# A decoder layer on one core: the attention steps of a quad taken chunk by chunk instead of pair by pair

## Chip, core and metric

The kernel runs on one core of a Trainium2 chip. The metric is the device time of one execution in microseconds (us). Engines are named as in the profile: PE is TensorE (PEld its weight loads), DVE is VectorE, ACT is ScalarE, POOL is GpSimd, SP is SyncE, which only issues DMAs here.

## What is computed

A decoder layer on x of 16 batches x 128 tokens x 1024, in three stages, each behind a layer norm and with a residual: latent attention with 32 heads (rotary part included), cross attention to a context, and a feed-forward stage of three layers with signed weights. The change touches the first stage alone. Cut to that stage:

```python
c_q = hidden_states @ w_q_down                    # 1024 -> 384
q_nope = (c_q @ w_q_up_nope)...                   # 32 heads x 128
q_rope = rope((c_q @ w_q_up_rope)...)             # 32 heads x 64
c_kv = hidden_states @ w_kv_down                  # 1024 -> 128, keys and values of all heads
k_rope = rope(hidden_states @ w_k_rope)
q_lat = einsum('bhsd,hdr->bhsr', q_nope, wuk)     # latent query, 128 per head
scores = q_lat . c_kv + q_rope . k_rope           # causal, softmax
out_lat = einsum('bhst,btr->bhsr', probs, c_kv)
out = einsum('bhsr,hdr->bhsd', out_lat, wuv)... @ w_out
x = x + out
```

## The kernel before, in words

`transform` is the first stage. Tokens lie in four chunks of 512 (`CHUNKS`, four batches each), two chunks make a group (`CPG` = 2, `GROUPS` = 2). Heads lie in eight quads of four heads, a quad in two pairs. Every large product is made in three matmul passes of split operands (`three_passes`, lines 66 to 70: high x high, high x low, low x high), so nearly every result leaves PSUM twice: ACT copies the high part out, DVE subtracts it to make the low part.

**Preparation** (PE lines 621 to 646). For each of four chunks in the order 2, 3, 0, 1, and each of eight slices `k` of 128 columns, PE transposes a slice two ahead (`turn_x`, bank `prep_turned`) and multiplies the current one into five banks (`project`, m = 0 to 4: three banks of queries `c_q`, one of keys, one of rope keys). ACT and DVE split each transposed slice into `hT_hi`, `hT_lo` (three slices of room) and, after `k` = 7, empty the five banks into `tok`. `BESIDE` puts other work at the end of some (chunk, k): the absorbed weights of the first heads (`"A"`: w_q_up_nope times w_uk of a pair, `"B"`: w_uv times w_out of one head), the rope queries of chunk 0 and its first latent queries. `load_w_down` brings the projection weights in four equal pieces of two slices; ACT cuts the high part (`cut_w_down`, 720), POOL the low part (894).

**Opening** (PE 648 to 663). What has to be ready before the loop: rope queries of the second chunk, the first two score tiles, two more latent queries, the first turned probabilities and values.

**Quads.** `quads` (247) runs the slots: quads 0 to 6 in a loop ("full", group 0, and they absorb the weights of the next quad and store them), quad 7 ("switch", tokens of group 1 are loaded), quads 8 to 14 in a loop ("later", group 1, weights loaded back), the last quad ("last"). A quad has eight steps; step s is one pair of heads, one chunk, and two of its four batches. `place(s)` (222) says which: before, pair 0 takes steps 0 to 3 (chunk 0, then chunk 1), pair 1 steps 4 to 7. In slot s PE issues, strictly in this order (`slot`, 665): turn of the probabilities of step s+1, scores of s+2, output of s (first batch), a latent query for two units ahead, values of s+1, output of s (second batch), then in two slots of a quad (`ROPE_AT`) the rope queries of the next quad, and in six of them (`ABSORB`) a piece of weights to absorb. ACT (861), POOL (934) and DVE (1150) follow the same slots in an order of their own.

**The two query banks.** Latent queries, rope queries and absorbed weights all go through two PSUM banks `qbank`, used in turn and numbered by `USE`: use n is written to bank n mod 2, and may start once use n-2 has been read out by DVE. Each reader adds 1 to the semaphore `q_taken` per use, with one exception: DVE's `rope` (1043 to 1056) reads both banks of a rope (uses n+1, n+2) in four products with cosine and sine, and adds 2 after the last of them:

```python
times(0, 0, cos)
times(1, 1, sin)
times(2, 0, sin)
times(3, 1, cos).then_inc(q_taken, 2)
```

PE's waits: `rope` waits for `taken` and `taken + 1` before its halves (558), `absorb_head` for `taken + n` before half n (542), `latent` for `taken` (548).

SP issues all DMAs in one order written out by hand (`preparation` 327, `full_quad` 390, `switch_quad` 414, `later_quad` 459): raw weights go into two ring buffers, absorbed weights to DRAM, rope queries through DRAM and back (`relayout`, 280), tokens and weights of group 1 back from DRAM.

Of the kernel before, what the change touches and what calls it, by code (L numbers as in the profile page):

```python
# [23 lines left out]
F32R = mybir.dt.float32r  # L24
# [6 lines left out]
P = 128  # L31
# [8 lines left out]
PAIR = 2  # L40
# [32 lines left out]
def transform(nc, x, w_down, w_heads, w_rope, consts, scratch, x1_d):  # L73
# [14 lines left out]
    PIECES, SLICES = 4, 3  # L88
# [3 lines left out]
    ROPE_AT = {2: 0, 4: 1}  # L92

    turns = [("x", 0), ("x", 1)]
    for g in range(KT * N):
        if g + 2 < KT * N:
            turns.append(("x", g + 2))
        if g % KT == 2 and g > KT:
# [6 lines left out]
              (3, 1): ("rope", 0), (3, 3): ("latent", 0), (3, 4): ("latent", 1)}  # L105
# [4 lines left out]
    USES_PREPARED, USES_OPENING, USES_FULL, USES_SWITCH, USES_LATER = 8, 8, 24, 16, 12  # L110

    ctx = ExitStack()
    with ctx:
# [19 lines left out]
        wqr = sb("at_wqr", [P, 2, WQR_W], F32R)  # L133

# [5 lines left out]
        pT_hi = sb("at_pT_hi", [P, CH], F32R)  # L140
        pT_lo = sb("at_pT_lo", [P, CH], F32R)
# [4 lines left out]
        with ExitStack() as early:  # L146
# [8 lines left out]
            stats = sb("pj_stats", [P, BPC, 2, 6], of=early)  # L155
# [6 lines left out]
        qlat1 = sb("at_qlat1", [P, 2, PAIR, CH], F32R)  # L162
# [5 lines left out]
        nmax = [sb(f"at_nmax{i}", [P, PARTS]) for i in range(2)]  # L168
        sums = [sb(f"at_sums{i}", [P, PARTS]) for i in range(2)]
        rsum = [sb(f"at_rsum{i}", [P, PARTS]) for i in range(2)]  # L170
# [14 lines left out]
        w_in = [sem(f"pj_w_in{j}") for j in range(PIECES)]  # L185
# [36 lines left out]
        def place(s):  # L222

            return (s // 2) // CPG % 2, (s // 2) % CPG
# [5 lines left out]
        def first_use_later(m):  # L230
# [3 lines left out]
        USE = {"full": [3 * s for s in range(STEPS)], "switch": [0, 3, 6, 9, 10, 13, 14, 15],  # L234
               "later": [0, 1, 2, 5, 6, 9, 10, 11], "last": [0, 1, 2, 3]}
# [4 lines left out]
        ABSORB = {0: ("B", 2, 0, 0), 1: ("B", 3, 0, 2), 3: ("A", 0, 1, 4), 5: ("B", 0, 1, 6), 6: ("B", 1, 1, 8),  # L240
                  7: ("A", 2, 1, 10)}
# [17 lines left out]
        def absorbed(kind, s):  # L259
            if kind == "full":  # L260
                return ABSORB.get(s)
            return ABSORB[s] if kind == "switch" and s < 2 else None

# [5 lines left out]
        def _(sp):  # L269
# [53 lines left out]
            def load_w_down(j):  # L323
                rows = slice(j * KT // PIECES, (j + 1) * KT // PIECES)
                sp.dma_start(w_raw[:, rows, :], w_down[:, rows, :]).then_inc(w_in[j], 16)

            def preparation():
# [4 lines left out]
                for t in range(BPC):  # L332
                    load_x_tile(0, t)
                load_w_down(0)
# [55 lines left out]
            def full_quad(q):  # L390

                parts, uses = USES_PREPARED + 12 * q, first_use(q)
                load_raw_rope(q + 1)
                sp.wait_ge(ab_mm, parts + 2)
                load_pair(q + 1, 0, 0)
                store_wqr(q + 1)
                sp.wait_ge(ab_mm, parts + 4)
                load_head(q + 1, 0, 1)
                store_wvo(q, 1, uses + USE["full"][1] + 3)
# [1403 lines left out]
```

## Time and profile before

| | |
|---|---|
| median of three runs | 2170.99 us (2170.54 to 2172.58) |
| the profiled execution | 2170.82 us |
| its span in the profile | 2168.7 us |
| mean granted PE clock | 0.985 |
| PE busy | 2088.7 us, 96% of the span, 10688 matmuls |
| DVE busy | 1278.7 us, 59% |
| ACT busy | 712.3 us, 33% |
| POOL busy | 361.9 us, 17% |

The span is the time from the first to the last instruction that the profiler saw; 2.1 us of the execution lie around it. Busy times of the engines overlap. In the timeline, the two numbers of a row are start and duration; matmuls are pipelined, so the next one starts before the record of the one before ends, and what a matmul costs the engine is the distance of two starts. A slot of a full quad is named by its step.

### The profile page before, as it was taken

The numbers are of one execution on the slowest core, as the hardware profiler recorded it, in microseconds if no ns is written. First come the engines' busy times: TensorE is split into PE (matmuls) and PEld (weight loads), VectorE is DVE, ScalarE is ACT, GpSimd is POOL, SyncE is SP. The second block draws the span as 40 slices with busy tenths as digits, with TensorE's granted clock in tenths as the row PEclk, the third lists the DMA queues.
The fourth block names the chain that finished last, engine by engine and source line by source line (L and its number), as shares of the span: only waits on it lengthen the run. The fifth ranks groups of instructions, "written<-read, shape, count | busy, mean of one in ns | idle before, by whom it ended". The sixth has DMA issues, their size and how long they took to land. (4 is left out here: it accounts for less than half of the span.)

```text
span 2168.7 us, 29831 instructions
## 1 busy us (share of the span) xinstructions
PE 2088.7 (96%) x10688; PEld 1741.3 (80%) x10688; DVE 1278.7 (59%) x2122; ACT 712.3 (33%) x1911; POOL 361.9 (17%) x316
## 2 busy tenths in 40 slices
PE   6998999999999999999999999999998869999999
PEld 4786888888888888888888888888887647888887
DVE  4645666666666666666666666666665764233322
ACT  3323343333333343333333333233332223232321
POOL 2011212122121212021121211212110114000000
PEclk9998999999999999999999999999999888999999
DMA  5624353543535443666433434324332971012000
GB/s 189 239 84 140 129 180 118 175 147 121 181 121 165 134 144 128 218 239 244 158 92 106 131 129 137 107 91 141 132 95 83 391 304 59 39 39 78 1 39 39
DMA packets 66695, 297.47 MB, mean 137 GB/s; under 512 B 6992, under 2 KB 7888, under 8 KB 55248
## 3 DMA queue, kind: packets, MB, share of 16 engines
q1 hardware_dynamic: 66640, 296.72, 39.5%
q8 instruction: 37, 0.61, 0.1%
q14 instruction: 18, 0.15, 0.0%
HBM read 179.25 MB, written 117.44 MB: 137 GB/s over the span
## 5 line engine op out<-in xcount | busy, mean ns | idle before, releaser
L1088 DVE TENSOR_TENSOR at_acc<-at_out,at_acc 128x512 f32<-128x512 f32 x512 | 351.8, 687 | 92.7 <-PE at_out L70 86.3
L70 PE MATMUL at_out<-at_wvo,at_val_lo 128*128 128x512 f32 x1024 | 401.5, 392 | 0.0
L68 PE MATMUL at_out<-at_wvo,at_val_hi 128*128 128x512 f32 x1024 | 401.1, 392 | 0.0
L69 PE MATMUL at_out<-at_wvo,at_val_hi 128*128 128x512 f32 x1024 | 400.7, 391 | 0.0
L787 ACT ACTIVATE at_probs<-at_probs,at_nmax 128x128 f32<-128x128 f32 x512 | 199.6, 391 | 419.9 <-DVE at_nmax L1066 419.9
L907 POOL TENSOR_TENSOR at_probs<-at_probs,at_rsum 128x512 f32<-128x512 f32 x128 | 133.4, 1042 | 857.3 <-DVE at_rsum L1071 857.3
L70 PEld LDWEIGHTS at_out<-at_wvo,at_val_lo 128*128 128x128 f32 x1024 | 192.7, 188 | 41.8
L68 PEld LDWEIGHTS at_out<-at_wvo,at_val_hi 128*128 128x128 f32 x1024 | 193.3, 189 | 32.5 <-DVE at_acc L1088 0.6
L69 PEld LDWEIGHTS at_out<-at_wvo,at_val_hi 128*128 128x128 f32 x1024 | 192.9, 188 | 31.4
L1697 PE MATMUL ff_lin<-ff_act_hi,ff_w 128*128 128x512 f32 x512 | 200.5, 392 | 6.1 <-DVE ff_act_lo L1632 6.1
L1698 PE MATMUL ff_lin<-ff_act_lo,ff_w 128*128 128x512 f32 x512 | 199.9, 390 | 0.0
L793 ACT ACTIVATE at_pT_hi<-at_turned 128x512 fp32r<-128x512 f32 x128 | 76.4, 597 | 322.3 <-PE at_turned L593 322.3
L586 PE MATMUL at_score<-at_tok,at_qrope 128*128 128x256 f32 x512 | 171.3, 335 | 0.0
L584 PE MATMUL at_score<-at_tok,at_qlat 128*128 128x256 f32 x512 | 154.8, 302 | 1.8 <-DMA at_qrope<-parts_d 1.8
L68 PE MATMUL at_qbank<-at_tok,at_wabs 128*128 128x512 f32 x384 | 151.2, 394 | 2.1 <-DVE at_rope_tmp L1049 2.1
L69 PE MATMUL at_qbank<-at_tok,at_wabs 128*128 128x512 f32 x384 | 151.6, 395 | 0.0
L70 PE MATMUL at_qbank<-at_tok,at_wabs 128*128 128x512 f32 x384 | 150.1, 391 | 0.0
L1639 DVE TENSOR_TENSOR ff_act_lo<-ff_hid,ff_act_hi 128x512 fp32r<-128x512 f32 x64 | 45.1, 708 | 174.1 <-ACT ff_act_hi L1587 174.1
L1040 DVE TENSOR_TENSOR at_qlat<-at_qbank,at_qlat 128x512 fp32r<-128x512 f32 x128 | 88.2, 689 | 88.8 <-ACT at_qlat L773 88.8
L914 POOL TENSOR_TENSOR at_rope_tmp<-at_rope_tmp 128x512 f32<-128x512 f32 x64 | 81.5, 1295 | 327.0 <-DVE at_rope_tmp L1049 327.0
L1697 PEld LDWEIGHTS ff_lin<-ff_act_hi,ff_w 128*128 128x128 f32 x512 | 96.6, 189 | 27.2 <-DVE ff_act_lo L1632 7.2
L585 PE MATMUL at_score<-at_tok,at_qlat 128*128 128x128 f32 x512 | 114.2, 223 | 0.0
(150 smaller groups left out, 3916.9 us busy)
## 6 DMA issues: line engine op xcount, KB each, us to landing
wvo_d<-at_wvo SPq DMA_DIRECT2D x16, 2048.0 KB, 8.0
parts_d<-at_rope_parts SPq DMA_DIRECT2D x32, 1024.0 KB, 6.4
at_qrope<-parts_d SPq DMA_DIRECT2D x128, 256.0 KB, 5.2
at_wvo<-wvo_d SPq DMA_DIRECT2D x16, 2048.0 KB, 8.4
ab_raw<-in_w_heads SPq DMA_DIRECT2D x32, 576.0 KB, 4.4
cr_ctx_raw<-in_context SPq DMA_DIRECT2D x16, 1024.0 KB, 9.2
wabs_d<-at_wabs SPq DMA_DIRECT2D x16, 768.0 KB, 7.0
at_wabs<-wabs_d SPq DMA_DIRECT2D x16, 768.0 KB, 7.7
```

Source lines behind the costliest of these rows:

```text
L68: pe.matmul(out, w_hi, x_hi, start=first, stop=False)
L69: pe.matmul(out, w_hi, x_lo, start=False, stop=False)
L70: return pe.matmul(out, w_lo, x_hi, start=False, stop=last)
L584: pe.matmul(score[:, j], q_hi, keys[:, :, cols], start=True, stop=False)
L585: pe.matmul(score[:, j, 0], q_lo, keys[:, 0, cols], start=False, stop=False)
L586: ins = pe.matmul(score[:, j], qrope[c][:, pair * PAIR + h, cols], rope_keys[:, :, cols], start=False, stop=True)
L787: ins = act.activation(probs[i][:, j, :], probs[i][:, j, :], ACT.Exp, bias=nmax[i][:, j:j + 1], accum_out=sums[i][:, j:j + 1])
L907: pool.tensor_tensor(probs[i][:], probs[i][:], rsum[i][:].unsqueeze(2).to_broadcast([P, PARTS, SEQ]), ALU.mult).then_inc(probs_ready, 1)
L1040: dve.tensor_tensor(qlat[u % 2][:, 1, h, :], qbank[use % 2][:], as_f32(qlat[u % 2][:, 0, h, :]), ALU.subtract).then_inc(q_taken, 1)
L1088: dve.tensor_tensor(at, outb[n][:], at, ALU.add).then_inc(added, 1)
L1697: pe.matmul(lin[m % 2][:], wk, act_hi[at][:, k, :], start=k == 0, stop=False)
L1698: ins = pe.matmul(lin[m % 2][:], wk, act_lo[at][:, k, :], start=False, stop=k == KT - 1)
```

## The change

The steps of a quad go chunk by chunk: both pairs on chunk 0 (steps 0 to 3), then both on chunk 1. With it:
- `ROPE_AT` puts the second rope of a quad behind slot 5 instead of slot 4, and `ABSORB` the six pieces behind slots 0, 3, 4, 5, 6, 7 instead of 0, 1, 3, 5, 6, 7. Slot 5 now has both, a rope and a head to absorb; `absorbing` gives the piece the bank uses behind those of the rope.
- The latent queries of both pairs on chunk 0 are made in the preparation (`BESIDE`), none in the opening; the opening absorbs head 2 of the first quad.
- The opening is put in another order on all engines.
- In the preparation, `turn_x` for two slices ahead is issued ahead of the slice's five projections instead of behind the first of them, and queries are emptied after the transposed slice.
- The projection weights come in pieces of 1, 1, 2 and 4 slices, the first right behind the first tile of x.
- SP's orders follow; some tiles lie elsewhere in SBUF; the small statistics share one tensor.

The diff, cut (places of tiles, and DVE's and ACT's loops where they repeat PE's, are left out):

```diff
-    PIECES, SLICES = 4, 3
+    SLICES = 3
+    PIECES = (slice(0, 1), slice(1, 2), slice(2, 4), slice(4, KT))
-    ROPE_AT = {2: 0, 4: 1}
+    ROPE_AT = {2: 0, 5: 1}
     BESIDE = {(0, 4): ("A", 0), (0, 6): ("A", 1), (1, 4): ("B", 0), (1, 6): ("B", 1),
-              (3, 1): ("rope", 0), (3, 3): ("latent", 0), (3, 4): ("latent", 1)}
+              (3, 1): ("rope", 0), (3, 3): ("latent", 0), (3, 4): ("latent", 1),
+              (3, 5): ("latent", 2), (3, 6): ("latent", 3)}
-    USES_PREPARED, USES_OPENING, USES_FULL, USES_SWITCH, USES_LATER = 8, 8, 24, 16, 12
+    USES_PREPARED, USES_OPENING, USES_FULL, USES_SWITCH, USES_LATER = 8, 10, 24, 14, 12
...
         def place(s):
-            return (s // 2) // CPG % 2, (s // 2) % CPG
+            return s // 2 % 2, s // UNITS % CPG
...
-        USE = {"full": [3 * s for s in range(STEPS)], "switch": [0, 3, 6, 9, 10, 13, 14, 15],
-               "later": [0, 1, 2, 5, 6, 9, 10, 11], "last": [0, 1, 2, 3]}
+        USE = {"full": [0, 3, 4, 7, 10, 13, 18, 21], "switch": [0, 3, 4, 7, 8, 9, 12, 13],
+               "later": [0, 1, 2, 5, 6, 7, 10, 11], "last": [0, 1, 2, 3]}
-        ABSORB = {0: ("B", 2, 0, 0), 1: ("B", 3, 0, 2), 3: ("A", 0, 1, 4), 5: ("B", 0, 1, 6), 6: ("B", 1, 1, 8),
-                  7: ("A", 2, 1, 10)}
+        ABSORB = {0: ("B", 3, 0, 0), 3: ("A", 0, 1, 1), 4: ("A", 2, 1, 2), 5: ("B", 0, 1, 3), 6: ("B", 1, 1, 4),
+                  7: ("B", 2, 1, 5)}
+        AHEAD, ITEMS = 5, 6
+        def absorbing(kind, s):
+            return USE[kind][s] + (3 if s in ROPE_AT else 1)
...
             def preparation():   # SP
-                for t in range(BPC):
+                load_x_tile(0, 0)
+                load_w_down(0)
+                for t in range(1, BPC):
                     load_x_tile(0, t)
-                load_w_down(0)
...
             def full_quad(q):    # SP
-                parts, uses = USES_PREPARED + 12 * q, first_use(q)
+                parts, uses = 2 * (AHEAD + ITEMS * q), first_use(q)
+                sp.wait_ge(ab_mm, parts)
+                load_pair(q + 1, 0, 0)
                 load_raw_rope(q + 1)
                 sp.wait_ge(ab_mm, parts + 2)
-                load_pair(q + 1, 0, 0)
+                load_pair(q + 1, 1, 1)
+                store_wvo(q, 1, uses + absorbing("full", 0) + 2)
                 store_wqr(q + 1)
+                relayout(q + 1, 0)
                 sp.wait_ge(ab_mm, parts + 4)
-                load_head(q + 1, 0, 1)
+                load_head(q + 1, 0, 0)
+                store_wabs(q + 1, 0, uses + absorbing("full", 3) + 2)
                 sp.wait_ge(ab_mm, parts + 6)
+                load_head(q + 1, 1, 1)
+                store_wabs(q + 1, 1, uses + absorbing("full", 4) + 2)
                 sp.wait_ge(ab_mm, parts + 8)
+                load_head(q + 1, 2, 0)
+                sp.wait_ge(ab_mm, parts + 10)
+                load_head(q + 1, 3, 1)
                 relayout(q + 1, 1)
+                store_wvo(q + 1, 0, uses + absorbing("full", 6) + 2)
...
             def project(i, m, k):    # PE
-                if m == 0:
+                if m == 0 and s + 2 >= KT * N:
                     pe.wait_ge(prep_turn_taken, turn_at["x", s] + 1)
...
                     for k in range(KT):
+                        if KT * i + k + 2 < KT * N:
+                            turn_x(KT * i + k + 2)
                         for m in range(5):
                             project(i, m, k)
-                            if m == 0 and KT * i + k + 2 < KT * N:
-                                turn_x(KT * i + k + 2)
-                            if m == 3 and k == 2 and i:
+                            if m == 2 and k == 2 and i:
                                 turn_kv(i - 1)
...
             def opening():   # PE
-                turn_kv(N - 1)
                 pe.wait_ge(down_taken, 5 * (N - 1) + QT)
-                rope(1, first + 4, first + 3)
                 scores(0, 0, 0, first + 4)
-                for h in range(PAIR):
-                    latent(1, h, first + 6 + h, first + 5 + h)
+                rope(1, first + 6, first + 5)
                 scores(0, 1, 0, first + 4)
                 pe.wait_ge(down_taken, 5 * N)
                 turn(0, 0)
+                turn_kv(N - 1)
+                values(0, 0, 0)
+                pe.wait_ge(ring_in[0], 48)
+                absorb_head(0, first + 8, first + 7)
                 pe.wait_ge(kr_lo, N)
                 pe.wait_ge(prep_turn_taken, turn_at["kv", N - 1] + 1)
-                values(0, 0, 0)
-                pe.wait_ge(q_taken, first + 8)
                 pe.wait_ge(val_lo_done, 1)
...
                     rope(ROPE_AT[s], use[s] + 1, first + use[s])     # PE, slot
                 if part := absorbed(kind, s):
-                    i = at // 2 % 2
-                    pe.wait_ge(ring_in[i], 16 * (3 * m + 3 + at // 4))
+                    i, bank_use = (AHEAD + at) % 2, absorbing(kind, s)
+                    pe.wait_ge(ring_in[i], 16 * (ITEMS // 2 * m + (AHEAD + at) // 2 + 1))
                     if what == "A":
-                        absorb_pair(i, use[s] + 1, first + use[s])
+                        absorb_pair(i, bank_use, first + bank_use - 1)
                     else:
-                        absorb_head(i, use[s] + 1, first + use[s])
+                        absorb_head(i, bank_use, first + bank_use - 1)
...
             def preparation():   # ACT
+                cut_w_down(0)
-                for t in range(2):
+                for t in range(BPC):
                     root(0, t)
                     first_normalise(t)
-                root(0, 2)
-                cut_w_down(0)
-                first_normalise(2)
-                root(0, 3)
-                first_normalise(3)
+                cut_w_down(1)
                 turn_x(0)
-                cut_w_down(1)
+                cut_w_down(2)
                 turn_x(1)
-                cut_w_down(2)
                 cut_w_down(3)
...
             def opening():   # ACT
                 rope_keys(N - 1)
+                exps(0, 0)
+                turn(0, 0)
+                exps(0, 1)
                 kv_values(N - 1)
-                exps(0, 0)
-                latent(0, 1, 0, first + 6)
+                values(0, 0)
                 rope(0, 1, 16)
-                latent(0, 1, 1, first + 7)
-                exps(0, 1)
-                turn(0, 0)
-                values(0, 0)
+                take_head(2, first + 8, 8)
...
-                rope_sums(first + 6)     # POOL, opening
+                normalise(0, 0)
+                rope_sums(first + 8)
+                normalise(0, 1)
                 rope_low(0, 1)
-                normalise(0, 0)
-                normalise(0, 1)
...
             def opening():   # DVE
-                rope_keys_low(N - 1)
-                kv_values(N - 1)
-                rope(0, 1, first + 4, 2)
                 largest(0, 0)
-                latent(0, 1, 0, first + 6)
-                latent(0, 1, 1, first + 7)
+                rope(0, 1, first + 6, 2)
                 recip(0, 0)
                 largest(0, 1)
+                turn(0, 0)
+                kv_values(N - 1)
                 recip(0, 1)
-                turn(0, 0)
                 values(0, 0)
+                take_head(2, first + 8, 8)
+                rope_keys_low(N - 1)
```

## Rows read from the trace of the kernel before

**Rows 1.** Page, busy tenths of 40 equal slices; PEclk in tenths.

```profile
PE   6998999999999999999999999999998869999999
...
PEclk9998999999999999999999999999999888999999
```

**Rows 2.** Waits of PE: total us, times, longest us.

```profile
PE at_value L68 <- DVE at_pT_lo L1075: 3.3, 1, 3.3
...
PE at_qbank L68 <- DVE at_rope_tmp L1049: 2.1, 1, 2.1
PE at_score L584 <- DMA at_qrope<-parts_d: 1.8, 1, 1.8
...
PE at_turned L593 <- DVE at_val_lo L1079: 1.7, 1, 1.7
PE at_turned L593 <- POOL at_probs L907: 1.3, 1, 1.3
PE at_qbank L534 <- DVE at_wabs L1028: 1.2, 1, 1.2
```

**Rows 3.** Stretches: length, busy PE, PEld, DVE, ACT, POOL, PEclk, DMA, GB/s.

```profile
43.66:47.07 3.41, 2.24 (x16) 1.89 (x15) 0.56 (x1) 0.97 (x2) 0.00 (x0) 1.00 0.00 0
173.35:176.76 3.41, 1.28 (x7) 0.92 (x7) 3.38 (x6) 0.38 (x1) 1.05 (x1) 1.00 0.54 217
176.76:180.18 3.42, 3.42 (x10) 2.65 (x9) 1.19 (x3) 2.47 (x10) 1.48 (x2) 0.50 0.00 0
187.00:200.66 13.66, 8.87 (x31) 7.44 (x31) 4.88 (x8) 2.59 (x8) 1.04 (x1) 0.50 0.45 106
200.66:892.00 691.34, 691.34 (x3616) 574.59 (x3615) 463.86 (x757) 253.18 (x731) 142.32 (x119) 1.00 0.45 146
```

**Rows 4.** Timeline of PE, slot 4 to 5, first full quad.

```profile
260.40 0.39 PE L70 MATMUL at_qbank<-at_tok,at_wqr 128*128 128x512 f32 x1
260.63 0.60 PE L593 MATMUL at_turned<-at_ident,at_probs 128*128 128x128 f32 x4
```

**Rows 5.** Timeline of DVE, then POOL, behind that rope.

```profile
260.93 0.69 DVE L1049 TENSOR_TENSOR at_rope_tmp<-at_qbank,at_cos 128x512 f32<-128x512 f32 x1 [3.60 <-PE at_qbank L70]
...
262.73 0.68 DVE L1049 TENSOR_TENSOR at_rope_tmp<-at_qbank,at_cos 128x512 f32<-128x512 f32 x1
...
269.38 2.53 POOL L921 TENSOR_TENSOR at_rope_parts<-at_rope_tmp,at_rope_parts 128x512 fp32r<-128x512 f32 x2 [0.31 <-ACT at_rope_parts L781]
```

**Rows 6.** Page, DMA issues: count, KB each, us to landing.

```profile
parts_d<-at_rope_parts SPq DMA_DIRECT2D x32, 1024.0 KB, 6.4
...
ab_raw<-in_w_heads SPq DMA_DIRECT2D x32, 576.0 KB, 4.4
```

**Rows 7.** Timeline of PE, then DVE, in the opening.

```profile
166.92 0.39 PE L70 MATMUL at_out<-pj_hT_hi,pj_w_lo 128*128 128x512 f32 x1
...
175.68 0.50 PE L68 MATMUL at_qbank<-at_tok,at_wabs 128*128 128x512 f32 x1 [2.13 <-DVE at_rope_tmp L1049]
...
174.95 0.68 DVE L1049 TENSOR_TENSOR at_rope_tmp<-at_qbank,at_cos 128x512 f32<-128x512 f32 x1
```

**Rows 8.** Timeline of DVE, then POOL, in the opening.

```profile
169.81 0.68 DVE L1010 TENSOR_TENSOR pj_k_rot<-pj_k_rot,pj_k_sin 64x512 f32<-64x512 f32 x1
...
183.19 1.04 POOL L907 TENSOR_TENSOR at_probs<-at_probs,at_rsum 128x512 f32<-128x512 f32 x1 [0.22 <-DVE at_rsum L1071]
```

**Rows 9.** Timeline of PE, then DVE, third slice of the second chunk.

```profile
70.94 0.63 PE L510 MATMUL at_out<-at_ident,pj_kv_raw 128*128 128x128 f32 x4 [0.31 <-DVE pj_hT_lo L981]
...
70.10 0.69 DVE L981 TENSOR_TENSOR pj_hT_lo<-at_out,pj_hT_hi 128x512 fp32r<-128x512 f32 x1
```

**Rows 10.** Timeline of PE, then ACT, at the start.

```profile
18.22 1.08 PE L503 MATMUL at_out<-at_ident,pj_x 128*128 128x128 f32 x4 [18.22 <-ACT pj_x L730]
...
23.40 1.08 PE L503 MATMUL at_out<-at_ident,pj_x 128*128 128x128 f32 x4 [0.22 <-DVE pj_hT_lo L981]
...
12.57 1.25 ACT L722 ACTIVATE pj_w_hi<-pj_w_raw 128x1280 fp32r<-128x1280 f32 x1
```

More of the change, by code:

```diff
@@ L133, in transform @@
         wqr = sb("at_wqr", [P, 2, WQR_W], F32R)
+        row_stats = sb("at_row_stats", [P, 3, 2, PARTS])
+        nmax, sums, rsum = ([row_stats[:, j, i] for i in range(2)] for j in range(3))
         with ExitStack() as early:
@@ L482, in _ @@
             last = GROUPS * QUADS - 1
-            for step in range(UNITS, STEPS):
+            for step in (2, 3, 6, 7):
                 c, b = place(step)[1], 2 * (step % 2)
@@ L673, in slot @@
                 if kind in ("full", "switch"):
-                    pe.wait_ge(q_taken, first + (use[1] + 3 if pair else -3))
-                elif s % UNITS == 0:
+                    pe.wait_ge(q_taken, first + (use[0] + 3 if pair else -3))
+                elif s in (0, 2):
                     pe.wait_ge(wvo_in[pair], 16 * (m - QUADS + 1))
@@ L844, in preparation @@
                             elif what == "latent":
-                                latent(0, 0, n, first + 2 + n)
+                                latent(0, n // 2, n % 2, first + 2 + n)
                         if (i, k) == (N - 1, 3):
                             rope(0, 0, None)
+                        if k == KT - 1:
+                            if i >= CPG:
+                                act.wait_ge(cq_out[i % CPG], 16)
+                            for m in range(QT):
+                                query(i, m)
+                            keys(i)
             def opening():
@@ L947, in _ @@
             ins.then_inc(zeroed, 1)
-            for j in range(PIECES):
+            for j in range(len(PIECES)):
                 cut_w_down(j)
@@ L1170, in slot @@
                 if part := absorbed(kind, s):
-                    what, h, ahead, at = part
+                    what, h, _, at = part
+                    count = 2 * (AHEAD + ITEMS * m + at)
                     if what == "A":
-                        take_pair(h // 2, use[s] + 1, USES_PREPARED + 12 * m + at)
+                        take_pair(h // 2, absorbing(kind, s), count)
                     else:
-                        take_head(h, use[s] + 1, USES_PREPARED + 12 * m + at)
+                        take_head(h, absorbing(kind, s), count)
             dve.sem_inc(added, 2)
```

125 lines of the change are left out of this document (51 added, 74 removed).

## The prediction

> **What bounds the kernel now.** First I read the page's slices [rows 1]: PE is at nine tenths or more nearly everywhere, with dents in the first slices, in the fourth (the opening, after about 165 us) and at the two later stage borders, which the change doesn't touch. The table of stretches then gives the loop: from 200.66 to 892 us PE is busy 691.34 of 691.34 us at full clock, seven full quads of 98.8 us each (691.34 / 7) [rows 3]. There is nothing to win there by reordering; a new wait in that stretch is paid in full, seven times. The list of PE's waits shows what can be won: five waits of the opening, 3.3 + 2.1 + 1.8 + 1.7 + 1.3 = 10.2 us [rows 2]. Third, the clock: after the 2.13 us gap of the opening [rows 7] PE ran at 1.2 GHz (0.50) for 3.42 us, and from 187.00 to 200.66 again with 8.87 us of work in it [rows 3]. At half clock the work takes twice its time, so this costs 3.42 / 2 = 1.7 and 8.87 / 2 = 4.4 us. The opening thus wastes 10.2 + 1.7 + 4.4 = 16.3 us. Everything PE computes is the same before and after: the number of matmuls doesn't change, so only waits and clock count.
>
> **Slot 5, the term that decides.** Before, no slot that ends with a rope also absorbs: behind the rope of slot 4 PE goes on with the next slot's turn, 0.23 us after the rope's last matmul (260.40, 260.63) [rows 4], and the next use of a query bank is one output (twelve matmuls) and more away. Now slot 5 has both. Its uses are: latent 13, rope 14 and 15, head 0 of the next quad 16 and 17. `absorb_head` waits for `q_taken` at first + 15; with the latent read out it stands at first + 14, and DVE's rope adds its 2 only behind the last of its four products. PE issues in order, so the head, and behind it the turn of step 7, the scores of the next quad's step 0, and all the rest wait for DVE's whole rope. Its length stands in the trace: DVE starts at 260.93, its last product ends at 262.73 + 0.68 = 263.41 [rows 5]. In the opening PE came back 0.05 us after the end of that same product (174.95 + 0.68 = 175.63, then 175.68) [rows 7]. PE would otherwise go on at 260.63, so a stall is 263.46 - 260.63 = 2.83 us, 2.9 with the slower first matmul behind a gap (0.50 against 0.39) [rows 4, 7]. Nothing hides it: DVE stood idle 3.60 us before the rope [rows 5], it can't start sooner, and the banks can't be given up sooner because products one and three read the first, two and four the second. Who else waits: ACT and DVE `take_head` come behind the absorb and move with it; POOL's rope sums don't. Only the full quads both rope and absorb in slot 5 (the switch quad absorbs at slot 0 alone, the later ones nothing): 7 x 2.9 = **+20.3 us**. Bounds: 7 x 2.5 = 17.5 (DVE's 2.48 alone) to 7 x 3.1 = 21.7.
>
> **The clock behind these stalls.** No row shows one inside the loop; the nearest are in the preparation and the opening. A gap of 1.2 us [rows 2] left the clock at 1.00 through 43.66 to 47.07; one of 2.13 us was followed by 3.42 us at 0.50 [rows 3]. A gap of 2.9 us is longer than either, so I expect a spell behind most: one costs 1.7 us, and I take 1.3 us a stall for the ones that escape, 7 x 1.3 = **+9.1 us**. Bounds: 0 (none) and 7 x 3.4 = 23.9 (two spells each, as in the long stretch of the opening, where clock and waits fed each other). The Trainium skill ("TensorE: Matmul & The Clock Gate", section "Why this matters for your kernels") advises only against idle gaps longer than about 3 us, which these are not: by it this term would be 0. The trace speaks against it: there 2.13 us were enough.
>
> **The opening.** Removed from it are two latent queries; they move behind slices 5 and 6 of the last chunk, at the price of the same matmuls. Added is head 2's absorption, taken out of the first quad's slot 0, again even. What changes is the waiting. Set T at the end of the projections (166.92 + 0.23 = 167.15) [rows 7]. PE now runs scores (1.4), rope (4.2) and scores (1.4) without a wait: the first needs only the queries, the third DVE's `largest`, which can run once DVE has rotated the keys at 169.81 + 0.68 = T + 3.3 [rows 8]. That is T + 7.2. DVE finishes the rope at about T + 8.5 and the reciprocal behind it, POOL normalises for 1.04 us [rows 8], so the turn starts at T + 9.9: 2.7 us idle. Behind it the split of the turned tile on ACT and DVE leaves 1.3 us. Then values and the head, and last `kr_lo`: DVE does `rope_keys_low` as the very last, behind exps, values and both parts of the head, 2.7 us after PE is done. The wait for the second chunk's rope queries from DRAM (1.8 us) [rows 2] goes, since step 2 is on chunk 0 and asks for none; the next one that does, step 4, is two slots later. Idle 6.7 us, and about 3.3 us more for slow clock behind gaps of this size (one to three spells of 1.7), together 10.0 against 16.3: **-6.3 us**. Bounds: -9.3 (no slow clock but 0.3) and -3 (3 us more of it).
>
> **Order of the preparation.** `turn_x` comes 0.69 us earlier (three matmuls), but at a chunk's border that does not make it land earlier: DVE's moments hold it. At the third slice of the second chunk PE waited 0.31 us for the low part that DVE ended at 70.10 + 0.69, then turned the keys at 70.94, with four projections of that slice done [rows 9]. Now it will have done three at the same time, because DVE and ACT are the same: 0.69 us lost, and some 0.25 us again one slice on. Twice (at the second and third chunk, which have moments beside them), and a little at the last: **+2.0 us**, bounds +0.3 and +2.5.
>
> **Start.** PE starts at 18.22, behind the last normalisation [rows 10]. The first cut of the weights now is one slice instead of two (ACT 1.25 us halved [rows 10]) and lies ahead of the normalisations, not between; I get PE's start some 0.6 us earlier. Against that, the first three projections no longer lie between the second and third transposition (23.40, 0.22 us idle), they come behind it, and cost 3 x 0.43 us at 1.2 GHz less the 0.22 us there plus some. Sum **+0.3 us**, bounds -1 and +2. The fourth piece (four slices) is needed at slice 4, over 10 us later: covered.
>
> **SP's order and the rest.** In slot 5 PE also waits for the raw head in ring 0. SP issues it behind slot 3 and the first `relayout`: POOL ends its low part at 269.38 + 2.53 = 271.91, 11.3 us into the slot after a rope, SP then sits 6.4 us on the copy to DRAM, and the head lands 4.4 us after issue [rows 5, 6]: some 24 us after slot 3 begins, and it is wanted two and a half slots (of 12 us on average) after that, about 31. Covered, 0 us; if it weren't, the spare of 7 us would have to be gone first. Loads of group 1 have two slots or more where they had so before. Taken at 0, bounds 0 and +2.
>
> **Sum.** 20.3 + 9.1 - 6.3 + 2.0 + 0.3 = +25.4 us on the profiled execution's 2170.82 us (0.2 us from the median): 2196.2, said as 2196 us. About 0.2% (4.3 us) is what a measurement here tells from no change.
>
> **Rivals.**
> *The clock holds.* The stalls come, no spell follows: 2170.8 + 20.3 - 6.3 + 2.3 = 2187. For it: no long busy stretch like the loop has a gap in the trace, the 2.13 us one had thin work around it [rows 3]. Against: the row itself. Chance 0.22. It is also what the advice in the Trainium skill's "TensorE: Matmul & The Clock Gate" would make of it.
> *Spells come double*, or stall and late ring add up: 9.1 becomes up to 23.9, 2203 to 2211. Chance 0.08.
> *The opening isn't shortened*, the change does not do what its order says: the wait for `kr_lo` at the end of DVE's chain eats what the others give, so -6.3 becomes 0: 2202. Chance 0.07.
> *The other side, no stall in slot 5.* If the absorb finds the banks free, all of 20.3 and 9.1 goes and 2170.8 - 6.3 + 2.3 = 2167 remains, down to 2164 with the opening's best bound. It decides at one point: whether DVE's rope is done when PE reaches the absorb. It would need 2.9 us of other work on PE between the rope and the head, and in the order of `slot` there is none. Chance 0.08.
>
> **Numbers.** Forecast (2196, own range 2190 to 2203) 0.55, the others 0.22, 0.08, 0.07, 0.08. Leaving out the no-stall case and the far end of the double spells, the range is 2184 to 2206. Faster by over 0.2% is half of the no-stall case, 0.05; within 0.2%, 0.04; slower 0.91.
>
> **What the profile after would show.** PE's waits: a new one of `at_qbank`, the absorb of a head, released by DVE's rope products, 7 times, 2.9 us each (none: the forecast falls). PEclk below 1.00 in the loop's stretch, about 12 to 20 us of it at 0.50 (none: the first rival). A full quad of 102 to 104 us instead of 98.8. In the opening waits of 6 to 7 us, none on the rope queries from DRAM, the last of them on DVE's low part of the keys. Two more waits of `prep_turned`, 0.3 to 0.7 us each, per chunk border. The forecast is wrong if the number of these waits isn't seven, or if slot 5 hides them.

## The result and the profile after

| | kernel before | kernel after |
|---|---|---|
| time, median (range) | 2171.77 us (2170.54 to 2172.58) | 2204.61 us (2203.24 to 2205.09) |
| ratio to before | 1 | 1.0151 (95%: 1.0133 to 1.0168) |
| profiled execution, its span | 2170.82, 2168.7 us | 2204.33, 2202.2 us |

The change made the kernel 33.5 us slower between the two profiled executions; 25.4 us were forecast. The page after, to be read against [rows 1]:

```profile
PE 2104.5 (96%) x10688; PEld 1745.1 (79%) x10688; DVE 1281.5 (58%) x2122; ACT 712.7 (32%) x1911; POOL 360.7 (16%) x316
...
PE   5999999999999999999999999999999778999999
...
PEclk9999999999999999999999999999999888999999
```

In tenths of 55 us nothing of it is to be seen: a gap of 2.7 us is a twentieth of a slice. The list of PE's waits (us in total, times, longest) shows it at once:

```profile
PE at_qbank L550 <- DVE at_rope_tmp L1049: 18.7, 7, 2.7
PE at_out L510 <- ACT pj_x L736: 18.2, 1, 18.2
...
PE at_out L510 <- DVE pj_hT_lo L981: 4.0, 7, 1.5
...
PE at_turned L600 <- POOL at_probs L907: 2.5, 1, 2.5
PE at_turned L600 <- DVE at_tok L1015: 2.2, 1, 2.2
PE at_out L517 <- DVE pj_hT_lo L981: 1.4, 3, 0.8
...
PE at_value L68 <- DVE at_pT_lo L1075: 0.6, 1, 0.6
```

The first line is new. It is slot 5 of the seven full quads: the absorption of a head waits for DVE's rope. The opening is down to 2.5 + 2.2 + 0.6 = 5.3 us in three waits, against 10.2 in five [rows 2]; `prep_turned` (L510, L517) has more, 4.0 + 1.4 us in ten waits against 1.7 + 0.6 us in four before. The timeline of the first full quad's slot 5 (start, length, engine and line, shapes, in brackets the idle time before it and its releaser) shows the stall itself:

```profile
268.68 0.40 PE L70 MATMUL at_qbank<-at_tok,at_wqr 128*128 128x512 f32 x1
269.20 0.69 DVE L1049 TENSOR_TENSOR at_rope_tmp<-at_qbank,at_cos 128x512 f32<-128x512 f32 x1 [3.60 <-PE at_qbank L70]
...
271.01 0.68 DVE L1049 TENSOR_TENSOR at_rope_tmp<-at_qbank,at_cos 128x512 f32<-128x512 f32 x1
271.74 3.19 PE L550 MATMUL at_qbank<-ab_raw 128*128 128x512 f32 x4 [2.67 <-DVE at_rope_tmp L1049]
```

PE's last rope matmul starts at 268.68, DVE's last product ends at 271.01 + 0.68 = 271.69, and 0.05 us later PE goes on. The four matmuls behind it then take 3.19 us. The loop and the three spells at low clock in it (window; its length; busy time and count of PE, PEld, DVE, ACT, POOL; granted clock, DMA share, GB/s), against the 1.00 without a break of [rows 3]; each window begins 0.2 us behind its spell, which is itself at 0.50:

```profile
197.50:950.00 752.50, 733.81 (x3768) 603.66 (x3767) 488.62 (x789) 265.85 (x769) 144.83 (x122) 0.99 0.43 146
272.55:275.96 3.41, 3.41 (x10) 1.79 (x9) 1.05 (x2) 1.33 (x3) 1.71 (x2) 0.52 0.00 0
477.35:484.18 6.83, 6.40 (x18) 4.23 (x19) 2.45 (x4) 1.79 (x3) 2.48 (x2) 0.51 0.21 45
583.16:586.58 3.42, 3.42 (x5) 1.33 (x6) 0.69 (x1) 0.60 (x1) 2.35 (x2) 0.53 0.00 0
```

Last, what no list of waits shows. In a quad of the second half, where slots 7 and 0 neither rope nor absorb nor wait, the turns (L593 before, L600 after) that open slot 7, the next slot 0 and slot 1 start here, first in the kernel before, then in the one after:

```profile
1237.56 0.60 PE L593 MATMUL at_turned<-at_ident,at_probs 128*128 128x128 f32 x4
...
1247.65 0.60 PE L593 MATMUL at_turned<-at_ident,at_probs 128*128 128x128 f32 x4
...
1257.73 0.60 PE L593 MATMUL at_turned<-at_ident,at_probs 128*128 128x128 f32 x4
```

```profile
1267.07 0.60 PE L600 MATMUL at_turned<-at_ident,at_probs 128*128 128x128 f32 x4
...
1277.16 0.60 PE L600 MATMUL at_turned<-at_ident,at_probs 128*128 128x128 f32 x4
...
1287.39 0.60 PE L600 MATMUL at_turned<-at_ident,at_probs 128*128 128x128 f32 x4
```

Slot 7 takes 10.09 us in both. Slot 0 takes 10.08 us before and 10.23 after, with PE busy throughout and the same matmuls. Slots on pair 1 are unchanged, slots on pair 0 (0, 1, 4, 5) cost about 0.15 us more; in them the 24 output matmuls of 128x512 take 5.61 instead of 5.48 us, 0.2336 instead of 0.2285 us from one to the next. The rest is in the nine latent matmuls (2.08 for 2.06 us) and the six of the values (0.72 for 0.70). On pair 1 the sum stays the same although its parts moved: values 0.72 for 0.70 there too, latents 2.04 for 2.06, though the two tiles of the latents (`wabs`, `tok`) lie where they lay. A later quad goes from 89.08 to 89.70 us (+0.62), a full one without a low-clock spell from 98.69 to 102.18 (+3.49, of which 2.87 is the stall).

**Where 33.5 us went.** Start of the first slot 0, of the switch quad and of the last quad, before and after: 191.59 and 193.38, 887.87 and 916.65, 1603.97 and 1635.96. The steps are thus +1.79, +26.99 and +3.21, and 1.50 in the last quad and behind it. One head of 1.71 us moved from the switch quad into the opening; without it they are +0.08, +26.99, +4.92, +1.50.

| term | forecast | measured | how |
|---|---|---|---|
| stall of slot 5 | +20.3 | +20.1 | 7 x (3.49 - 0.62) |
| low clock behind it | +9.1 | +6.4 | 26.99 - 7 x 3.49 + 3.8 |
| opening and its tail | -6.3 | -6.7 | -2.9 to slot 0, -3.8 in the first quad (5.4 over a full quad of 98.69 before; after, without its spell of low clock, 1.6 over 102.18) |
| start and order of the preparation | +0.3, +2.0 | +3.0 | the third projection of the last slice at 165.11 and 172.25, less two latents of 2.07 |
| slots on pair 0 | none | +9.6 | 7 x 0.62 in the full quads, 4.92 from the switch quad to the last, 0.33 in the last |
| cross attention and feed-forward | 0 | +1.2 | 1.50 - 0.33 |

The terms are rounded singly; unrounded they add up to 33.5. The split of a full quad's 3.49 us takes the 0.62 of a later quad; by the run free below, whose full quad takes 99.24 us, it is 2.94 and 0.55, that is 20.6 us of stall and 9.1 of slots on pair 0.

### The profile page after: what moved, and what is told of

Same layout as the page of the kernel before. It is cut to its first block and busy times, and to the rows that moved or that the text cites. A ratio compares the mean times of both kernels' runs of the same rounds, so it can differ in the third digit from the quotient of the medians.

```text
span 2202.2 us, 29822 instructions
## 1 busy us (share of the span) xinstructions
PE 2104.5 (96%) x10688; PEld 1745.1 (79%) x10688; DVE 1281.5 (58%) x2122; ACT 712.7 (32%) x1911; POOL 360.7 (16%) x316
## 5 line engine op out<-in xcount | busy, mean ns | idle before, releaser
L793 ACT ACTIVATE at_probs<-at_probs,at_row_stats 128x128 f32<-128x128 f32 x512 | 199.5, 391 | 403.8 <-DVE at_row_stats L1066 403.8
L907 POOL TENSOR_TENSOR at_probs<-at_probs,at_row_stats 128x512 f32<-128x512 f32 x128 | 133.1, 1040 | 900.6 <-DVE at_row_stats L1071 900.6
L593 PE MATMUL at_score<-at_tok,at_qrope 128*128 128x256 f32 x512 | 171.7, 335 | 0.0
L779 ACT ACTIVATE at_qlat<-at_qbank 128x512 fp32r<-128x512 f32 x128 | 75.9, 593 | 120.3 <-PE at_qbank L70 120.3
```

The source lines that it names most:

```text
L593: ins = pe.matmul(score[:, j], qrope[c][:, pair * PAIR + h, cols], rope_keys[:, :, cols], start=False, stop=True)
L793: ins = act.activation(probs[i][:, j, :], probs[i][:, j, :], ACT.Exp, bias=nmax[i][:, j:j + 1], accum_out=sums[i][:, j:j + 1])
L907: pool.tensor_tensor(probs[i][:], probs[i][:], rsum[i].unsqueeze(2).to_broadcast([P, PARTS, SEQ]), ALU.mult).then_inc(probs_ready, 1)
```

## The experiments

In all of them the ratio is to the kernel before on the same chip. The kernel after was not measured beside them, and before's own median lies between 2170.15 and 2171.77 us from case to case, so a difference to the 2204.61 of the kernel after is good to 1 or 2 us only. Where it matters, the same stretch of the two traces is compared as well. Theory A (the prediction's): the absorption behind a rope in slot 5 stalls PE seven times, and the clock falls behind these stalls. Theory B: the stall or its size belongs to the order chunk by chunk. Theory C, formed from the table above: matmuls slow down because tiles moved in SBUF. The change puts the small statistics of the softmax (`nmax`, `sums`, `rsum`) into one tensor declared early, so the later tiles lie 96 bytes further on (`pT` and `qlat1` have besides changed places).

### b_rope5: the kernel before, with only the second rope moved to slot 5

```diff
-    ROPE_AT = {2: 0, 4: 1}
+    ROPE_AT = {2: 0, 5: 1}
-        USE = {"full": [3 * s for s in range(STEPS)], "switch": [0, 3, 6, 9, 10, 13, 14, 15],
-               "later": [0, 1, 2, 5, 6, 9, 10, 11], "last": [0, 1, 2, 3]}
+        USE = {"full": [0, 3, 6, 9, 12, 13, 18, 21], "switch": [0, 3, 6, 9, 10, 11, 14, 15],
+               "later": [0, 1, 2, 5, 6, 7, 10, 11], "last": [0, 1, 2, 3]}
...
+        def absorbing(kind, s):
+            return USE[kind][s] + (3 if s in ROPE_AT else 1)
```

> The kernel before, pair by pair, with only the second rope moved from slot 4 to slot 5 and head 0 absorbed behind it. If rope and absorb in one slot are the stall: seven PE waits on DVE's rope of 2.7 us, a full quad 2.8 us longer, 19.8 us plus 0 to 12 us of slow clock, 2192 to 2204 us. If the chunk order makes the waits: no such wait, 2172 us.

Measured: 2223.14 us, ratio 1.0239 (1.0222 to 1.0257), above the range expected. PE's waits:

```profile
PE at_score L587 <- DMA at_qrope<-parts_d: 19.0, 9, 2.2
PE at_qbank L546 <- DVE at_rope_tmp L1052: 18.7, 7, 2.7
```

The same seven waits of the same size, in the order pair by pair: the stall is the rope's place beside an absorption, not the new order. What I had missed is the line above it. Pair by pair, step 2 is on chunk 1, and its scores, issued in slot 0 of the next quad, need chunk 1's rope queries from DRAM, three slots after a rope in slot 5. The order chunk by chunk gives these transfers two more slots. So a rope in slot 5 is cheaper in the new order; in the old one it costs another 17 us of waits: the kernel before has one of the nine (1.8 us, in the opening), the eight others, 2.0 to 2.2 us each, open the quads of the second half. Low clock followed five of these eight gaps and four of the seven of 2.7 us.

### filled: the kernel after, with twelve matmuls laid into the stall

```diff
                     rope(ROPE_AT[s], use[s] + 1, first + use[s])
+                    if kind == "full" and s == 5:
+                        for k in range(12):
+                            pe.matmul(turned[:], wqr[:, 0, 0:P], tok[:, 0, CQ_HI:CQ_HI + CH], start=True, stop=True)
```

The results of these matmuls are not used.

> The changed kernel with twelve matmuls more in slot 5 of a full quad, between rope and absorb, into the free turned bank; their result is not used. They fill PE's wait (12 x 0.23 = 2.76 us) and take none of it away. If the wait let the clock fall: no spell at 1.2 GHz in the loop, 6.8 us less than the changed kernel's 2204.6, about 2198 us. If the spells have another cause: 2204 to 2206 us.

Measured: 2198.10 us, 1.0124 (1.0107 to 1.0140), 6.5 us under the kernel after. The slot 5 of above, and the loop's window:

```profile
269.74 2.96 PE L712 MATMUL at_turned<-at_tok,at_wqr 128*128 128x512 f32 x12
272.57 1.98 PE L550 MATMUL at_qbank<-ab_raw 128*128 128x512 f32 x4
```

```profile
197.50:950.00 752.50, 752.50 (x3884) 621.61 (x3884) 490.46 (x793) 266.48 (x770) 145.00 (x122) 1.00 0.43 146
```

Slot 5 is as long as in the kernel after where that has no spell (19.09 us in both), since DVE's rope still has to end, but PE has no gap, the clock never falls in the loop, and the absorption behind it takes 1.98 us instead of 3.19. In the loop alone, from the first slot 0 to the switch quad, it is 716.93 against 723.27 us: the low clock costs 6.3 us, and the two causes are separated. The kernel after had three spells of together 13.65 us at 0.5 behind seven gaps of 2.7 us; at half clock that is at most 13.65 / 2 = 6.8 us of work lost, less a little for the time in which PE stood idle. The Trainium skill ("TensorE: Matmul & The Clock Gate", section "Why this matters for your kernels") advises against idle gaps longer than about 3 us. These were shorter and cost clock; here the advice is too lax.

### swap: the kernel after, with the absorption ahead of the rope in slot 5

```diff
+                if part := absorbed(kind, s):
+                    ...
+                        absorb_head(i, bank_use, first + bank_use - 1)
                 if s in ROPE_AT and end > STEPS:
                     ...
-                    rope(ROPE_AT[s], use[s] + 1, first + use[s])
-                if part := absorbed(kind, s):
-                    ...
-                        absorb_head(i, bank_use, first + bank_use - 1)
+                    rope(ROPE_AT[s], roping(kind, s), first + roping(kind, s) - 1)
```

> The changed kernel with head 0 absorbed ahead of the rope in slot 5, on PE and DVE alike, with the bank uses exchanged. The rope's first half then waits for the head's first bank: ACT and DVE have it 2.4 us after the absorb starts, PE is there after 1.7 us. If the stall is the hand-over of the query banks: 0.7 us of wait instead of 2.7, a gap that leaves the clock alone, so 7 x 2.1 + 6.8 = 21.5 us less than 2204.6, about 2183 us. If rope and head in one slot stall whatever their order (ring, ACT, DVE too full): as the changed kernel.

Measured: 2184.12 us, 1.0063 (1.0046 to 1.0080), 20.5 us under the kernel after, and 21.3 in the loop alone (702.02 against 723.27 us). Its wait, and the row in the first full quad:

```profile
PE at_qbank L68 <- DVE at_wvo L1039: 3.9, 7, 0.6
```

```profile
266.97 0.50 PE L68 MATMUL at_qbank<-at_tok,at_wqr 128*128 128x512 f32 x1 [0.55 <-DVE at_wvo L1039]
```

Seven waits of 0.6 us stay, now the rope's for the absorbed head's read-out, and no spell of low clock. In this slot the second of the two uses waits either way; which of them goes second decides for how long: 2.7 us if four products on DVE have to end, 0.6 if a short split has.

### free: the kernel after, with no absorption in a slot that ropes

```diff
-        ABSORB = {0: ("B", 3, 0, 0), 3: ("A", 0, 1, 1), 4: ("A", 2, 1, 2), 5: ("B", 0, 1, 3), 6: ("B", 1, 1, 4),
-                  7: ("B", 2, 1, 5)}
-        AHEAD, ITEMS = 5, 6
+        ABSORB = {0: ("B", 2, 0, 0), 1: ("B", 3, 0, 1), 3: ("A", 0, 1, 2), 4: ("A", 2, 1, 3), 6: ("B", 0, 1, 4),
+                  7: ("B", 1, 1, 5)}
+        AHEAD, ITEMS = 4, 6
```

SP's loads, the counts of uses and the opening (which absorbs no head) follow from it.

> The changed kernel with nothing absorbed in slot 5: heads 2 and 3 in slots 0 and 1, pairs in 3 and 4, heads 0 and 1 in slots 6 and 7; the opening absorbs nothing. If rope and absorb in one slot are the stall: no wait in the loop, 19.8 us of waits and 6.8 us of slow clock less than 2204.6, 0 to 2 us back in the opening, 2178 to 2180 us. If a piece now comes too late from DRAM or a bank too late elsewhere: waits on other lines, over 2185 us.

Measured: 2176.23 us, 1.0026 (1.0016 to 1.0036). No wait in the loop, no low clock, a full quad of 99.24 us. Stall and clock are gone with one table: between the spans of the two traces (2202.2 and 2174.4) it is 27.8 us, of which 7 x (102.18 - 99.24) = 20.6 are the stall, 6.4 the clock and 0.7 the opening. It is still slower than before although the opening has kept part of what it won: 99.24 - 98.69 = 0.55 us a quad is left that no wait explains, and that is theory C's.

### b_stats, b_wvo, b_val: the kernel before, with only tiles moved

b_stats moves the small statistics to where the kernel after has them; the two others put 96 bytes of padding in front of one tile each.

```diff
         wqr = sb("at_wqr", [P, 2, WQR_W], F32R)
+        row_stats = sb("at_row_stats", [P, 3, 2, PARTS])
...
-        nmax = [sb(f"at_nmax{i}", [P, PARTS]) for i in range(2)]
-        sums = [sb(f"at_sums{i}", [P, PARTS]) for i in range(2)]
-        rsum = [sb(f"at_rsum{i}", [P, PARTS]) for i in range(2)]
```

```diff
+        wvo_pad = sb("at_wvo_pad", [P, 24])
         wvo1 = sb("at_wvo1",
```

```diff
+        val_pad = sb("at_val_pad", [P, 24])
         val_hi = [sb(f"at_val_hi{i}"
```

> The kernel before with only the six small statistics tiles gathered into one behind wqr, so that all later tiles, the value tiles among them, lie 96 bytes higher. If the 0.14 us that slots 0, 1, 4, 5 of the changed kernel cost more comes from where the tiles lie: slots 0 to 3 (pair 0) grow from 10.08 to about 10.23 us, a quad by 0.56 us, 16 quads 9 us, 2181 us. If it comes from the chunk order: 2172 us.

> The kernel before with the 96 unused bytes ahead of wvo1 alone: the value tiles stay. If it is the distance of value tile and wvo tile: now slots 0 to 3 (pair 0) stay at 10.08 us and slots 4 to 7 (pair 1) take 10.23 us, 2180 us. If the value tiles' own place is the cause: all slots at 10.08, 2171 us.

> The kernel before with 96 unused bytes ahead of the value tiles: val, qrope1 and wvo1 lie 96 bytes higher, all else where it was. If an output matmul is slowed by how the value tile (its weights) lies against the wvo tile (its moving operand): pair 0, whose wvo0 stays, takes 10.23 us a slot instead of 10.08, pair 1, whose wvo1 moves along, stays at 10.08; 2180 us as in b_stats. If another of the moved tiles is the cause: 2171 us.

Measured: b_stats 2179.58 us, 1.0040 (1.0026 to 1.0054); b_wvo 2179.33, 1.0038 (1.0024 to 1.0051); b_val 2174.57, 1.0017 (1.0008 to 1.0027). None has a PE wait that the kernel before hasn't. The turns of slot 7, slot 0 and slot 1, as above, in b_stats (L592), b_wvo and b_val (L594):

```profile
1242.52 0.60 PE L592 MATMUL at_turned<-at_ident,at_probs 128*128 128x128 f32 x4
...
1252.61 0.60 PE L592 MATMUL at_turned<-at_ident,at_probs 128*128 128x128 f32 x4
...
1262.85 0.60 PE L592 MATMUL at_turned<-at_ident,at_probs 128*128 128x128 f32 x4
```

```profile
1242.46 0.60 PE L594 MATMUL at_turned<-at_ident,at_probs 128*128 128x128 f32 x4
...
1252.68 0.60 PE L594 MATMUL at_turned<-at_ident,at_probs 128*128 128x128 f32 x4
...
1262.79 0.60 PE L594 MATMUL at_turned<-at_ident,at_probs 128*128 128x128 f32 x4
```

```profile
1238.17 0.60 PE L594 MATMUL at_turned<-at_ident,at_probs 128*128 128x128 f32 x4
...
1248.24 0.60 PE L594 MATMUL at_turned<-at_ident,at_probs 128*128 128x128 f32 x4
...
1258.43 0.60 PE L594 MATMUL at_turned<-at_ident,at_probs 128*128 128x128 f32 x4
```

b_stats has the kernel after's 10.09 and 10.24 us, with nothing else changed. That is the missing term: its ratio is worth 8.7 us, the ledger had 9.6. b_wvo turns it round: with `wvo1` shifted against the values slot 7, on pair 1, takes 10.22, pair 0 10.08 to 10.11. In its slot 7 the output matmuls alone are slower (0.2336 us apart; latents and values as before). Taken together the two say that the place of `wvo` relative to `val` counts: in b_stats `val` and `wvo1` both move by 96 bytes and pair 1 keeps its pace, while in each run the pair whose two tiles moved apart loses it. b_val shows the direction for pair 0 (10.19) but came out at 2174.6 where 2180 was expected, because its pair 1 slots (10.02 to 10.07) were faster than before's (10.08 to 10.10) and its value matmuls, whose tiles this run leaves in place, keep before's 0.117 us where b_stats and the kernel after have 0.120. That the latter are slower too, where `pT` has moved against `tok`, makes them a second pair of tiles whose place matters. b_val also moves `qrope1` and `wvo1`, and what made pair 1 faster is open.

### free_pad: free, with val and all behind it on by 416 bytes more

```diff
+        val_pad = sb("at_val_pad", [P, 104])
         val_hi = [sb(f"at_val_hi{i}"
```

> free with 416 unused bytes ahead of the value tiles: together with the 96 of the statistics they lie 512 bytes higher than before, so their distance from wvo0 is a multiple of 512 bytes again. If only the distance matters: pair 0's slots fall back to 10.09 us, a full quad from 99.24 to 98.7 us, free's 2176.2 less 9 is 2167 us. If any shift of the value tiles slows them: 2176 us.

Measured: 2170.34 us, 0.9999 (0.9990 to 1.0009), 5.9 us under free; 2167 was expected. With a shift of 512 bytes instead of 96 a full quad takes 98.90 us (before 98.69, free 99.24) and a later one 89.38: a half to two thirds of the cost are gone, not all, and all slots are now alike at 10.12 to 10.13. The output matmuls are 0.2296 us apart on both pairs, and the value matmuls 0.1195: `pT` still lies 96 bytes on. Pair 1, whose `val` and `wvo1` keep their old distance here, is slower than before (10.13 for 10.09). So a multiple of 512 restores the old pace only roughly, the distance of the two tiles isn't the whole rule, and the rule stays open.

### prep_old: the kernel after, with the old order of the preparation

```diff
-                        if KT * i + k + 2 < KT * N:
-                            turn_x(KT * i + k + 2)
                         for m in range(5):
                             project(i, m, k)
+                            if m == 0 and KT * i + k + 2 < KT * N:
+                                turn_x(KT * i + k + 2)
```

ACT and DVE likewise split the next tile again between the first query and the others.

> The changed kernel with the preparation's old order on PE, ACT and DVE: transposition behind the first projection of a slice, the first query bank emptied ahead of it. If that order cost 0.68 us at each of two chunk borders and some at the last chunk, as the traces of before and after have it: last projection of the preparation 2.2 to 2.9 us earlier, and 0.7 at the first slices; 2201 to 2203 us. If the loss comes from the start alone (pieces, first loads): only 0.7 us less.

Measured: 2196.78 us, 1.0129 (1.0112 to 1.0146), below the range expected. The first matmul of the third projection of the last slice, in the kernel after and in this one:

```profile
172.25 0.39 PE L68 MATMUL at_turned<-pj_hT_hi,pj_w_hi 128*128 128x512 f32 x1
```

```profile
168.67 0.39 PE L68 MATMUL at_turned<-pj_hT_hi,pj_w_hi 128*128 128x512 f32 x1
```

The order costs 3.6 us: 1.5 at the first slices, 0.6 to 0.7 at each of two borders, 0.9 at the last chunk. Of the other 4 us of its gain most is not the preparation's: this kernel's loop had 6.8 us at low clock and the kernel after's 13.65, and was 3.3 us shorter. Nor is the clock the same from one execution to the next: three of this kernel's four took 2195.4 to 2196.8 us at a mean granted clock of 0.987, the fourth 2201.81 at 0.984.

### best: free_pad with the old preparation, the x tiles loaded ahead of the weights, and the low part of the keys earlier on DVE

Besides, ACT cuts all weight pieces behind the normalisations, and DVE waits for the cosine and sine tables only at their first use.

```diff
-                load_x_tile(0, 0)
-                load_w_down(0)
-                for t in range(1, BPC):
+                for t in range(BPC):
                     load_x_tile(0, t)
+                load_w_down(0)
...
                 turn(0, 0)
+                rope_keys_low(N - 1)
                 kv_values(N - 1)
                 recip(0, 1)
                 values(0, 0)
-                rope_keys_low(N - 1)
```

> free_pad with the preparation in its old order (transposition behind the first projection), the four weight pieces cut behind the normalisations, the wait for the tables put off to their first use, and the low part of the last rope keys earlier on DVE. Terms: order of the preparation 2.2 us, start 0.7 (back to before) plus 1.8 (no cut between the normalisations), opening 0.7. If these terms are right: free_pad less 5.4, about 2162 us, below the kernel before by 0.4%. If the start is held by the DMAs of the weights or the opening by another chain: 2164 to 2166 us.

Measured: 2164.55 us, 0.9970 (0.9959 to 0.9981), faster than both kernels; 2162 was expected. PE starts 2.2 us earlier than after's 18.2:

```profile
15.94 1.09 PE L510 MATMUL at_out<-at_ident,pj_x 128*128 128x128 f32 x4 [15.94 <-ACT pj_x L735]
```

So a kernel with the chunk order and the earlier queries can win: 6.6 us over the kernel before, once the absorption is off the roping slot, the tiles are near their old pace and the old preparation is back. Of the 5.8 us between free_pad and this kernel the start gives 2.2; how the rest divides was not measured singly. By the traces it is 7.2 us ahead of free_pad at the end of the preparation, 7.9 at the first slot 0, 7.5 behind the first quad and 6.7 at the end of the span: nearly all of it lies in the preparation.

## Why the prediction was nearly right, point by point

The time fell just above the forecast case's own range (2190 to 2203) and inside the whole one (2184 to 2206): mechanisms and sign were right, one term was missing. That the range held it is in part luck: its room was meant for the clock and the opening, and 9.6 us of a term that stood at nothing were partly covered by 2.7 us less of low clock than forecast. Of the other rivals none came true: the low clock was less than forecast and not double, the opening did get shorter, and slot 5 did stall.

- **What bounds the kernel** (right): the loop had no slack, and every microsecond put into it was paid seven times.
- **Slot 5** (right): seven waits, released by DVE's last product 0.05 us before PE went on, 20.1 us for 20.3. b_rope5 shows it without the change's order; swap and free take it away, by the order inside the slot and by the slot.
- **Clock** (mechanism right, size high): 6.3 to 6.4 us for 9.1. The 1.3 us a stall assumed a spell behind most gaps; there was one behind three of seven, one of them of double length. The bounds of 0 and 23.9 held it. The rival in which the clock holds (2187) falls with filled: without gaps 2198.1, with them 2204.6.
- **Opening** (right in its sum): -6.7 for -6.3. The waits came to 5.3 us where 6.7 were forecast, and the low clock, with 5.66 + 3.41 us of work in its two spells, to some 4.5 us where 3.3 were forecast; the two errors cancel. Its three waits:

```profile
184.24 1.09 PE L600 MATMUL at_turned<-at_ident,at_probs 128*128 128x128 f32 x4 [2.49 <-POOL at_probs L907]
...
186.74 0.58 PE L68 MATMUL at_value<-at_pT_hi,at_tok 128*128 128x256 f32 x1 [0.56 <-DVE at_pT_lo L1075]
...
193.38 0.69 PE L600 MATMUL at_turned<-at_ident,at_probs 128*128 128x128 f32 x4 [2.18 <-DVE at_tok L1015]
```

  Forecast were 2.7, 1.3 and 2.7. The last is for DVE's low part of the keys, as said, and none is left for rope queries from DRAM.
- **Preparation and start** (somewhat low): +3.0 for 2.0 + 0.3. At the fourth projection of the first slice the kernel after is 0.7 us behind (27.42 against 26.73), for 0.3 forecast, whose terms (-0.6 and 3 x 0.43 - 0.22) add up to 0.5; 2.3 us more are lost from there to the last slice, for 2.0. The border waits were named (0.3 to 0.7 us each, the first row below). By prep_old the order costs 3.6 in all, of which 1.5 at the first slices, which the forecast had under the start. PE's own start was off: it began at 18.16 and not 0.6 earlier, as DVE waited for the second tile of x, behind the weight piece that now goes ahead of it:

```profile
71.66 0.63 PE L517 MATMUL at_out<-at_ident,pj_kv_raw 128*128 128x128 f32 x4 [0.30 <-DVE pj_hT_lo L981]
```

```profile
9.40 1.29 DVE L958 BATCH_NORM_STATS2 pj_stats<-pj_x 128x6 f32<-128x512 f32 x2 [2.40 <-DMA pj_x<-in_x]
```

- **SP's order and the rest, taken at 0 to +2** (the step that failed): the loads were indeed covered (the prediction's "some 24 us" there are 11.3 + 6.4 + 4.4 = 22, which only adds to the spare), but the part asked only what is waited for. It rests on the sentence in which the prediction says that the number of matmuls doesn't change, "so only waits and clock count": that is false, since the time of one matmul changed. A tensor declared earlier was read as bookkeeping; it moved the later tiles by 96 bytes in SBUF and cost 8.7 us by b_stats, 9.1 to 9.6 by the ledger, more than the clock. b_stats shows it alone. The table of waits can't show such a term. Of the 1.2 us behind the loop the waits tell this much: PE's at `cr_turned` went from 13.1 + 2.6 to 17.6 us, its longest at `ff_turned` from 17.4 to 16.5; why was not looked into.

## What to carry to other kernels

A resource handed back by a semaphore is handed back by its last reader: where two uses of one pair of banks meet in a slot, put the one that is read out fastest first, and cost the other order as the whole read-out times the number of rounds (2.7 against 0.6 us here, seven times, and clock on top). A change that "only" moves or merges tiles need not be free where the bound engine streams from SBUF: compare the pace of identical, unstalled stretches before and after, then run the old kernel with the new places alone.

## What the runs showed of the hardware that I had not expected

A shift of 96 bytes between the tile that a 128x512 matmul takes its weights from and the one that it streams changed the pace from 0.2285 to 0.2336 us a matmul, 8.7 us over the kernel in b_stats (all that the shift does there), without a wait in the trace. It shows where the weights' tile moved and the streamed one stayed (b_stats, b_val, pair 0) and the other way round (b_wvo, pair 1), and a shift of 512 bytes took 5.9 us of it back. The mechanism is open: the trace gives only the distance of two starts. In slot 7 of a later quad the output matmuls of the kernel before settle at 0.227 us, those of b_wvo go 0.231, 0.238, 0.231 over and over. Something is also carried over from one group to the next: the latents' tiles moved in no run, and in that slot they are 0.226 to 0.231 us apart in the kernel after and up to 0.235 in the kernel before. The Trainium skill ("SBUF — State Buffer", section "Who interferes with whom") gives TensorE two read ports of its own, one for the moving operand and one for weight loads, independent of each other. By that the place of one operand relative to the other shouldn't matter; b_stats and b_wvo show that it does. Whether the two reads share something behind the ports, no run here tells.

The clock is less predictable than the gap before it. Seven gaps of 2.7 us, each with the same work around it, were followed by low clock three times, and the kernel after had twice the low-clock time (13.65 us) of a sister with the same stalls (6.8 us in prep_old). Nor does it take 2.7 us: in b_rope5 gaps of 2.0 to 2.2 us, with PE busy for a whole quad between them, were followed by low clock five times in eight, while the seven gaps of 0.6 us in swap never were. A term for it wants a range, not a value.
